# Graph attention over 50 source tiles: GpSimd scales a batch's messages in two halves, and TensorE waits for each half

## What is computed

```python
q_dst, k_src, v_src = Q[dst], K[src], V[src]          # 8 heads of 16
score = jnp.clip(jnp.sum(q_dst * k_src, -1) / sqrt(16), -5.0, 5.0)
attn = softmax(score, axis=0)                          # over all edges, per head
h_out = zeros.at[dst].add(attn[..., None] * v_src)
```

## Time and profile before

| what | value |
|---|---|
| median of 3 runs | 5492.09 us (5488.76 to 5493.91) |
| the profiled execution | 5486.88 us |
| its span in the trace | 5485.0 us |
| attention block (first line-1519 instruction to the last) | 1093.3 to 2975.3 us |
| granted TensorE clock in that block | 1.00 |

### The profile page before, as it was taken

How to read it: one execution, slowest core, us unless ns; L and a number is a source line. 1 busy time by engine, 2 the same in 40 slices (tenths; PEclk the granted TensorE clock), 3 DMA queues, 4 the chain that set the end, 5 groups by cost and what they waited for, 6 DMA issues and landing times. The chain is left out here.

```text
span 5485.0 us, 164969 instructions
## 1 busy us (share of the span) xinstructions
PE 5016.6 (91%) x56178; PEld 4464.3 (81%) x56254; DVE 4408.0 (80%) x7721; ACT 3289.6 (60%) x5897; POOL 1958.7 (36%) x1946
## 2 busy tenths in 40 slices
PE   5888888799999999999997869999999997899996
PEld 4777777699999999999997759999999996656555
DVE  8999992277777777777776659999999996588886
ACT  3444443377777777777774437777777773466651
POOL 3433345533333333333332445555555552300000
PEclk9999999899999999999998979999999998899988
DMA  4443431222222222222221123333333331000000
GB/s 161 155 147 147 153 138 55 77 99 93 90 96 91 93 90 97 90 94 93 90 98 46 40 75 128 133 129 132 127 132 127 130 129 33 0 1 0 0 0 24
DMA packets 175998, 498.05 MB, mean 91 GB/s; under 512 B 24861, under 2 KB 61728, under 8 KB 169500
## 3 DMA queue, kind: packets, MB, share of 16 engines
q1 hardware_dynamic: 169528, 491.34, 25.3%
q10 hardware_dynamic: 6372, 5.43, 0.3%
HBM read 466.39 MB, written 30.33 MB: 91 GB/s over the span
## 5 line engine op out<-in xcount | busy, mean ns | idle before, releaser
L1555 PE MATMUL ps<-kv_table,stage 128*128 128x256 bf16 x7203 | 1180.0, 273 | 29.7 <-ACT stage L1461 29.5
L1864 POOL TENSOR_TENSOR parts<-rest 128x512 bf16<-128x512 f32 x588 | 654.0, 1118 | 613.3 <-DVE rest L1923 607.0
L2062 PE MATMUL ps<-a_table,stage 128*128 128x128 bf16 x7203 | 794.6, 219 | 41.2 <-DVE stage L1899 41.2
L2065 PE MATMUL ps<-window,stage 128*128 128x128 bf16 x7350 | 812.1, 219 | 0.0
L1558 PE MATMUL ps<-window,stage 128*128 128x128 bf16 x7350 | 810.8, 219 | 0.0
L1519 POOL TENSOR_TENSOR message<-message 128x512 f32<-128x512 f32 (+1 forms) x441 | 445.5, 1010 | 899.1 <-ACT message L1468 899.1
L1387 DVE TENSOR_TENSOR product<-ps,q_kept 128x512 f32<-128x512 f32 (+1 forms) x637 | 426.3, 669 | 376.0 <-ACT message L1447 303.2
L1445 ACT ACTIVATE q_kept<-ps 128x512 f32<-128x512 f32 (+1 forms) x637 | 369.7, 580 | 544.8 <-PE ps L1558 536.6
L1555 PEld LDWEIGHTS ps<-kv_table,stage 128*128 128x128 bf16 x7203 | 629.5, 98 | 69.2 <-issue 30.3
L1558 PEld LDWEIGHTS ps<-window,stage 128*128 128x128 bf16 x7350 | 616.9, 98 | 55.9
L1981 ACT ACTIVATE parts<-ps 128x512 bf16<-128x512 f32 x588 | 349.1, 594 | 335.9 <-PE ps L2065 335.3
(11 more groups left out here) (368 smaller groups left out, 10876.9 us busy)
## 6 DMA issues: line engine op xcount, KB each, us to landing
stage<-lists SPq DMA_DIRECT2D x294, 768.0 KB, 4.0
edges<-in_edge_attr SPq DMA_DIRECT2D x49, 2240.0 KB, 8.3
stage<-lists SPq DMA_DIRECT2D x98, 896.0 KB, 5.5
window<-qkv_rows SPq DMA_DIRECT2D x49, 288.0 KB, 5.4
window<-ab_rows SPq DMA_DIRECT2D x49, 192.0 KB, 5.0
qkv_rows<-kv_table SPq DMA_DIRECT2D x21, 384.0 KB, 2.5
qkv_rows<-q_parts SPq DMA_DIRECT2D x21, 192.0 KB, 2.0
ab_rows<-a_table SPq DMA_DIRECT2D x21, 192.0 KB, 2.0
```

Source lines behind the costliest of these rows:

```text
L1555: nc.tensor.matmul(kv_ps[n % 2][:, i, :], from_src, kv_table[:, tile, q, :], start=(q == 0), stop=(q == 2))
L1864: pool.tensor_tensor(parts_of(n)[:, 0:nt, D:2 * D], rest[BUFFER[n]][:, 0:nt, :], middle[BUFFER[n]][:, 0:nt, :], ALU.subtract).then_inc(low ...
L2062: nc.tensor.matmul(to[:, i, :], from_src, a_table[:, tile, q, :], start=(q == 0), stop=False)
L2065: last = nc.tensor.matmul(to[:, i, :], own, window[d][:, (3 + q) * D:(4 + q) * D], start=False, stop=(q == 2))
```

## The change

GpSimd's one multiplication of a batch becomes two, over the first and the second half of its tiles (two and two, or one and one in the last batch of a group), each with an increment of `message1`. The scatter waits for the first increment ahead of its first tile and for the second ahead of the tile at the middle.

```diff
@@ scale (POOL) @@
-                        values = message[n % 3][:, 0:nt, 0:D].rearrange("p t (h c) -> p t h c", c=HEAD)
-                        pool.tensor_tensor(values, values, message[n % 3][:, 0:nt, D:D + HEADS].unsqueeze(3)
-                                           .broadcast_to([P, nt, HEADS, HEAD]), ALU.mult).then_inc(message1, 1)
+                        for t0 in (0, nt // 2):
+                            t1 = t0 + nt // 2
+                            values = message[n % 3][:, t0:t1, 0:D].rearrange("p t (h c) -> p t h c", c=HEAD)
+                            pool.tensor_tensor(values, values, message[n % 3][:, t0:t1, D:D + HEADS].unsqueeze(3)
+                                               .broadcast_to([P, nt // 2, HEADS, HEAD]), ALU.mult).then_inc(message1, 1)
@@ scatter (PE) @@
-                        pe.wait_ge(message1, s + 1)
+                        pe.wait_ge(message1, s * 2 + 1)
                         pe.wait_ge(slot_hot1, s + 1)
                         if b == 0:
                             pe.wait_ge(added1, j + 1)
                         for i, tile in enumerate(batch_tiles(b)):
+                            if 2 * i == len(batch_tiles(b)):
+                                pe.wait_ge(message1, s * 2 + 2)
                             last = nc.tensor.matmul(ps[:, 6 + d, 0:D + HEADS], slot_hot[n % 2][:, i, :],
                                                     message[n % 3][:, i, :], start=(tile == 0), stop=(tile == SELF))
                         last.then_inc(scattered1, 1)
```

## The result

The changed kernel takes 5450.5 us (median of four runs, 5447.1 to 5454.7) against 5491.2 before: ratio 0.9926, interval 0.9909 to 0.9943. Forecast were 5459 us and a range from 5451: the direction and the mechanism held, but the time fell 0.5 us outside the range. The four runs lie on both sides of 5451, and by the interval the time could be anywhere from 5441 to 5460 us, so on which side of the range's end it fell is within the scatter. What has to be explained are the 8.5 us beyond the forecast. Ratios are given as recorded; they can differ by up to 0.001 from the quotient of the two medians.

A forecast was written before the change was run, and what follows sets the result against it. TensorE was taken as the bound, GpSimd's latency mattering only at two holes a group. 49 x (0.34 - 0.05 + 0.38) = 33 us off the 5492.1 us median gave 5459 us, range 5451 to 5481.

The forecast's parts named there:

- the base: Kernel before: median 5492.1 us, from which 33 us are taken to give 5459; its profiled execution was 5486.9.
- The two holes: TensorE's waits ahead of the scatters of batches 10 and 0: 0.84 and 0.38 us too long, in 49 groups.
- GpSimd: Multiplication: halves of 0.62 us (one tile about 0.40), the second starting 0.07 before the first ends; signals at 0.62 and 1.18.
- The late start of 0.18: Rival: GpSimd's second half starts 0.18 us behind the first; gain only 13 us, 5479 us; chance 0.12.
- Batch 10: Gather behind its scatter starts at 1.69 instead of 2.03 us: gain 0.34, less 0.05 for waits behind the second release.
- Batch 0: Scatter starts at 0.80 without a hole, next gather at 1.72 instead of 2.10 us: gain 0.38 us.
- The added wait: Middle of all 637 scatters: met, so taken as free; rival says 0.07 us each, 45 us, time 5502; chance 0.05.
- no hole: Two-tile batch: scatter starts at 0.86, middle at 1.09, second half ends at about 0.74 us, so TensorE does not stand.
- The far price of 0.07 us for a wait: TensorE's upper cost for a wait queued behind an unmet one, from 0.12 against 0.05 us at batches 0 and 10.
- VectorE beside GpSimd: Line 1378 took 1.42 us beside GpSimd's multiplication, 0.62 without; after the change they still miss each other by 0.13.
- The block's sum: Attention block: 49 x (0.34 - 0.05 + 0.38) = 33 us shorter; profiled execution 5454 us.
- All other blocks the same: Everything outside the attention block was to keep its time; only that block would be 33 us shorter.

The follow-up runs named there:

- the two-batches run: Changed kernel with halves and middle wait at batches 0 and 10 of a group only, the other eleven in one instruction and one wait: 5454.1 us, ratio 0.9932.
- the three sets: Eleven follow-up kernels on three chips, each set beside its own executions of the kernel before, whose medians were 5487.1, 5489.0 and 5488.5 us.

## Why the prediction was right or wrong

The time left the range at its lower end. The mechanism and the terms of the block stood, and their sum came out 1.6 us too large, which moves the time the other way. The step that failed is the base; one sentence on everything outside the block failed too, by an amount about which less is known.

- **The two holes**: right. 49 at batch 10 and 48 at batch 0 in the trace of before; the two-batches run shows that nothing else is won.
- **GpSimd**: the second half starts 0.04 us before the first ends; I took 0.07 from the pair of line 278. The late start of 0.18 is out. The halves take 0.62, those of one tile 0.40.
- **Batch 10**: forecast gain 0.34 less 0.05, measured 2.03 - 1.74 = 0.29. The 0.05 was an even choice inside a bound, and that it came out is luck in part; 0.02 came from the second signal (third tile at 1.25 instead of 1.23) and 0.03 from the sequencer, whose five waits take 0.49 us where two tiles take 0.46. **Batch 0**: forecast 0.38, measured 0.38. From scatter to scatter batch 10 gained 0.32, since the gather behind a late start is 0.04 shorter, and batch 0 with the loop's end ahead of it 0.33: 49 x 0.65 = 32 us.
- **The added wait**: taken at nothing. True behind eight loads; alone it cost 0.10 us at 21 loop ends. In the changed kernel the step there is 0.12 longer, 2.5 us in all, by the two-tile message that ends later. For that batch the prediction said "no hole" and did not look at the jump. The far price of 0.07 us for a wait was too low; in sequence they stand about 0.10 us apart.
- **VectorE beside GpSimd**: that the two hold each other up by 0.8 us rests on one row, the block's first. In the same trace the 25 other instructions of line 1378 that run beside GpSimd's do so for 0.13 us at most and are no longer than the rest, and lines 1387 and 1391 run beside it for 0.4 to 0.6 us in most batches at their usual 0.69. What made the first one longer is not shown; nothing in the sum rested on it.
- **The block's sum**: 33 us forecast, 31.4 measured. For the profiled execution the forecast said 5454 and the first saw 5453.1; the other two saw 5446.7 and 5456.3, so that so close a figure is luck.
- **The base** ("5492.1 - 33 = 5459 is the forecast for the median"): failed. The median of three runs, 5492.1, stood 5.0 us above that of 21, and 3.6 above that of its 52 executions in the result and the three sets (5488.5). The profiled execution (5486.9), which I had set aside as 5.2 below, was the better estimate. The range covered costs of the change but no scatter of the base; an end lower by these 4 to 5 us would have held the result.
- **"All other blocks the same"**: failed in the traces. `layer1_nodes` was 5.2 us shorter (235.1 to 229.9, means of two and three traces), with fewer stretches at half clock, `layer2_edges` 3.8 shorter and `layer3_edges` 2.9 longer; all of the rest 4.8 shorter. Whether that belongs to the change or to the scatter of executions is not shown. With these: 5488.5 - 31.4 - 4.8 = 5452.3; the 14 executions of the changed kernel have a median of 5449.9, so 2 us stay unplaced.

What stays open is whether the shorter rest follows from the change at all, and the half-clock rounds from the time at which the block begins; a kernel with an empty delay ahead of it was not tried.

## What to carry to other kernels

Price a stall by the chain behind it and by TensorE's own order, hole for hole: two batches in thirteen held all of the gain, and a step as plain as 0.22 against 1.06 us between weight loads gave it to within 0.05 us a batch. Ask of each signal that comes later what its wait had covering it: two tiles and a jump were too little here. When an unmet wait stands ahead of met ones, put it last: the reordering of five waits won another 0.2 us a group, and with exp between the copies the kernel was 60 us faster in all. And give the base its own width: with three runs of before, several us of the forecast belonged to no mechanism.

## What the runs showed of the hardware that I had not expected

- A met wait on TensorE costs nothing behind eight fp32 loads and their matmuls (steps of 0.92 us with or without it), but about 0.10 us where nothing covers it: five behind the last release took 0.48 us, one more 0.11, two less saved 0.20.
- A message that was 0.14 us later ahead of a scatter of two tiles and a jump back made the step there 0.12 us longer and more (0.55 to between 0.67 and 0.76), though the scatter itself started on time; with 1.0 us to spare the step was 0.46.
- Splitting finer lost 18 us although GpSimd had idle time left between all batches; 11 of them are TensorE's way through batch 10, where its sequencer worked off waits behind one last tile.
- Executions of one kernel agree to 0.6 us in a block at full clock that lasts 1851 us, while a block of 230 us behind it differs by 4.3 us among the same three, and a round of it that meets a stretch at a granted clock of 0.50 takes 3.2 us more.
